# Layer-norm statistics: bf16 copy from GpSimd to ScalarE, square from ScalarE to VectorE

## What is computed

```python
x = x + 0.5 * ffn(_layernorm(x), Wg, We_gate, We_up, We_down, Ws_gate, Ws_up, Ws_down, Wsg)
x = x + attn(_layernorm(x), Wq, bq, Wk, bk, Wv, bv, Wo, bo)
x = x + 0.5 * ffn(_layernorm(x), ...)

def _layernorm(x, axis=-1, eps=1e-5):
    m = jnp.mean(x, axis=axis, keepdims=True)
    v = jnp.var(x, axis=axis, keepdims=True)
    return (x - m) / jnp.sqrt(v + eps)
```

## Time and profile before

| | us |
|---|---|
| median of three runs | 4568.49 |
| lowest, highest of the three | 4275.07, 4841.87 |
| the profiled execution | 4274.95 |
| its span, slowest core (core 2) | 4273.4 |
| spans of the eight cores | 4267.4 to 4273.4 |
| PE busy | 3931.2 |
| DVE busy | 2094.3 |
| ACT busy | 719.7 |
| POOL busy | 254.3 |

### The profile page before, as it was taken

One profiled execution on the slowest core, in us unless ns is written; L12 is line 12 of the kernel. 1 busy time (PEld: TensorE's weight loads), 2 busy tenths in 40 slices (PEclk: granted clock), 3 DMA queues, 4 the chain that ended last, 5 costly groups with the idle time before them and its releaser, 6 DMA issues.

```text
span 4273.4 us, 50465 instructions; the slowest of 8 cores (4267.4 to 4273.4 us)
## 1 busy us (share of the span) xinstructions
PE 3931.2 (92%) x17496; PEld 1592.7 (37%) x17496; DVE 2094.3 (49%) x3297; ACT 719.7 (17%) x1281; POOL 254.3 (6%) x390
## 2 busy tenths in 40 slices
PE   4699999999999999996878669999999999999999
PEld 1234444444444444431322223444444444444443
DVE  3545554445555555454334554555554445555544
ACT  3111111111111111113233321111111111111111
POOL 4100000000000000002000210000000000000000
PEclk7799999999999999997888779999999999999999
DMA  6023222232223222230020301321122211322112
GB/s 128 1 30 47 33 40 30 31 49 40 30 30 43 37 40 30 30 50 10 1 30 1 50 1 30 50 40 30 30 39 41 40 30 30 50 36 35 30 30 89
DMA packets 122599, 154.28 MB, mean 36 GB/s; under 512 B 3568, under 2 KB 93680, under 8 KB 122352
## 3 DMA queue, kind: packets, MB, share of 16 engines
q0 software_dynamic: 113744, 134.27, 21.1%
q1 hardware_dynamic: 6528, 12.59, 0.9%
q10 hardware_dynamic: 2080, 4.19, 0.3%
HBM read 276.91 MB, written 8.39 MB: 67 GB/s over the span
## 4 chain that ended last, share of the span: by engine, by line
PE 88%; DVE 5%; issue 3%; ACT 2%; DMA 1%; POOL 1%; DVEq 0%; ACTq 0%; POOLq 0%; SPq 0%
PE pb L534 27%; PE pb L576 27%; PE pb L558 26%; PE pb L657 1%; PE pb L824 1%; PE pb L646 1%; PE pb L567 1%; DVE t L393 1%; DVE rows L366 1%; DMA x_sb<-x_T 1%; DVE xn L397 1%; ACT t L757 0%; PE pb L343 0%; PE pb L348 0%; ACT t L760 0%
## 5 line engine op out<-in xcount | busy, mean ns | idle before, releaser
L534 PE MATMUL pb<-h_w,slab 128*128 128x512 bf16 x5120 | 1210.9, 378 | 41.5 <-DVE x_sb L539 4.4
L558 PE MATMUL pb<-xn,slab 128*128 128x512 bf16 x5120 | 1229.1, 384 | 0.0
L576 PE MATMUL pb<-xn,slab 128*128 128x512 bf16 x5120 | 1224.7, 382 | 0.0
L584 DVE TENSOR_TENSOR scr<-sg,w_sb 128x512 f32<-128x512 bf16 x640 | 442.8, 692 | 1280.7 <-ACT sg L581 1280.7
L539 DVE TENSOR_TENSOR x_sb<-x_sb,pb 128x512 f32<-128x512 f32 x1280 | 880.6, 688 | 345.2 <-PE pb L534 343.8
L558 PEld LDWEIGHTS pb<-xn,slab 128*128 128x128 bf16 x5120 | 505.2, 99 | 617.3 <-issue 26.4
L534 PEld LDWEIGHTS pb<-h_w,slab 128*128 128x128 bf16 x5120 | 433.6, 96 | 792.9 <-issue 412.9
L576 PEld LDWEIGHTS pb<-xn,slab 128*128 128x128 bf16 x5120 | 490.5, 98 | 612.0 <-issue 51.2
L581 ACT ACTIVATE sg<-pb 128x512 bf16<-128x512 f32 x640 | 381.3, 596 | 1315.9 <-PE pb L558 1315.8
L587 DVE TENSOR_TENSOR h_w<-scr,pb 128x512 bf16<-128x512 f32 x640 | 440.3, 688 | 163.4 <-PE pb L576 135.5
L572 ACT ACTIVATE w_sb<-pb 128x512 f32<-128x512 f32 x160 | 95.5, 597 | 1656.2 <-PE pb L567 1656.2
(11 more groups left out here) (116 smaller groups left out, 1032.3 us busy)
## 6 DMA issues: line engine op xcount, KB each, us to landing
slab<-WegT POOLq DMA_DIRECT2D x32, 1024.0 KB, 11.1
slab<-WeuT POOLq DMA_DIRECT2D x32, 1024.0 KB, 15.7
slab<-WedT POOLq DMA_DIRECT2D x32, 1024.0 KB, 9.5
slab<-WsgT POOLq DMA_DIRECT2D x8, 1024.0 KB, 11.0
slab<-WsuT POOLq DMA_DIRECT2D x8, 1024.0 KB, 15.1
slab<-WsdT POOLq DMA_DIRECT2D x8, 1024.0 KB, 9.2
out_T<-x_sb SPq DMA_DIRECT2D x4, 2048.0 KB, 7.1
x_sb<-x_T ACTq DMA_DIRECT2D x2, 2048.0 KB, 24.4
```

Source lines behind the costliest of these rows:

```text
L534: P.op("pe", lambda e, kc=kc, oc=oc, bd=bd, par=par: e.matmul(pb[bd][:, :], slab_d(4, kc, oc), h_w[:, par, kc, :], start=(kc == 0), stop=( ...
L558: P.op("pe", lambda e, sg_i=sg_i, kc=kc, hc=hc, t=t, bg=bg: e.matmul(pb[bg][:, :], slab_g(sg_i, kc, hc), xns(kc, t), start=(kc == 0), stop ...
L576: P.op("pe", lambda e, su_i=su_i, kc=kc, hc=hc, t=t, bu=bu: e.matmul(pb[bu][:, :], slab_g(su_i, kc, hc), xns(kc, t), start=(kc == 0), stop ...
L584: P.op("dve", lambda e, hc=hc: e.tensor_mul(t2f[:, :], sg[:, hc % 2, :], w_sb[:, :]), reads=[("sg", hc % 2), ("wsb",)], writes=[("scr32",)])
```

## The change

In `stats`, the bf16 copy of x moves from POOL to ACT, and the square moves from ACT to DVE, where it is made from the bf16 copy in `t2` instead of the float32 x. The buffers, their number, the matmuls and the recorded order stay.

```diff
-                    P.op("pool", lambda e, kc=kc, t=t, sl=sl: e.tensor_copy(
-                        t2[:, sl], xs(kc, t)),
+                    P.op("act", lambda e, kc=kc, t=t, sl=sl: e.activation(
+                        t2[:, sl], xs(kc, t), AF.Copy),
                         reads=[("x", kc, t)], writes=[tk])
-                    P.op("act", lambda e, kc=kc, t=t, par=par: e.activation(
-                        t1[:, par, :], xs(kc, t), AF.Square),
-                        reads=[("x", kc, t)], writes=[("t1", par)])
+                    P.op("dve", lambda e, kc=kc, sl=sl, par=par: e.tensor_mul(
+                        t1[:, par, :], t2[:, sl], t2[:, sl]),
+                        reads=[tk], writes=[("t1", par)])
```

## The result

The changed kernel takes 4318.2 us, the median of ten runs (lowest 4315.32); the kernel before, in ten runs beside it, 4275.33 (lowest 4274.72). The ratio is 1.0099, 95% interval 1.0087 to 1.0111: 1% slower, 43 us, and so within the 2% band. Forecast were 4317.0 and a range of 4290 to 4350. The profiled execution after took 4315.32 (span 4313.7, slowest core 6), 40.4 more than the 4274.95 of before (slowest core 2).

The account below looks back on a forecast made before the run. PE was seen busy 92% of the span, the change touching only three layer norms, each a chain over ACT and DVE. 12.5 + 3.4 + 3.1 + 22.8 = 41.8 us on 4274.95 gave 4317, range 4290 to 4350.

Parts of the forecast that it names:

- expert stages unchanged: Sign expected in the changed profile: the expert stages after the layer norms stay the same to a few us.
- The blocks, 22.8: Blocks 1 and 2 of each of three layer norms: row mathematics behind the multiplies, 3.8 us a block, 22.8 in all.
- The multiply at 0.42: Layer norms: each square on DVE takes 0.42 us with POOL idle, 0.87 as the upper end.
- Rival B: Layer norms: the DVE multiply takes 0.87 us, 16 us more than forecast, total 4333; chance 0.11.
- Block 0 in the attention and the second FFN, 3.4 and 3.1: Layer norms of attention and second FFN: the first root comes 3.4 and 3.1 us later, multiplies waiting behind DVE's residual add.
- Block 0 in the first FFN, 12.5: First layer norm: multiplies wait behind L310, so the root moves from 38.19 to 50.7 with a table load, 11.2 without.
- L310's place: Program start: DVE's first instruction, waiting for bias loads, moves from 32.63 to about 34.7 because early weight DMAs share bandwidth.
- the 4.1 us: Program start: q1 and q10's remaining 835 packets after 27 us, to the landing at 31.1; 6.2 with a third queue.
- rival C: Program start: the weights take more of the DMA engines, 6 us more, 4323, or up to 4354; chance 0.11.
- The stretches behind at no change: Stages after the three layer norms: no difference in length, 0 us in the sum.
- Rival A: Layer norms: not slower, since DVE is only 49% busy and the row mathematics stays hidden, 4275; chance 0.09.
- Rival D: Experts: longer gaps leave PE at its lower clock far in, slower by over 2%, 4360 and up; chance 0.04.

Follow-up runs that it names:

- e4: Changed kernel with the four DVE row operations L356 to L362 recorded one by one between the next block's multiplies: 4295.1 us, ratio 1.0048.
- e5: Kernel before with only the square moved to DVE, reading the bf16 copy, the cast staying on POOL: 4314.2 us, ratio 1.0091.
- e2: Changed kernel with the first weight slab DMA on POOL held until x's last block and the bias arrays have landed: 4305.8 us, ratio 1.0072.
- e11: Changed kernel with 12 added tiny DVE operations (copies of L310) ahead of expert 1's first token block in the first FFN: 4318.5 us, ratio 1.0099.
- e12: Changed kernel with 40 added tiny DVE operations (copies of L310) ahead of expert 1's first token block in the first FFN: 4321.2 us, ratio 1.0107.
- e6: Kernel before with only the cast moved to ACT, the square staying on ACT and reading float32 x: 4301.8 us, ratio 1.0061.

## Where the prediction was right, and which step failed

The forecast of 4317.0 lies 1.2 below the median and its direction, mechanism and places were right. That it lies so close is partly luck. The layer norms cost 4.1 more than forecast, and the stretches behind them, put at nothing, gave back 5.6. The step that failed in the layer norms is the price of the early weight DMAs, "With a third queue of equal share these become 6.2, so L310 runs at about 34.7": 2.1 us forecast, 5.5 measured. The step that failed behind them is "expert stages unchanged", with no term in the sum.

- **The blocks, 22.8.** Right. The six spacings that should grow did so by 4.07, 3.34, 3.47, 3.95, 4.05 and 3.40, 22.3 in all. Of each 3.8, the forecast had 2.8 for the row mathematics and 1.0 for the slower start and pace of the pairs; by the order alone e4 brought 16.7 of the 22.3 back, 2.8 a block, and 0.9 a block stayed. L356 stands right behind the last L340, as written.
- **The multiply at 0.42.** Right: 0.416 to 0.427 for all 96, with POOL not computing beside it; in e5, with POOL's casts there, the longest took 0.877. Rival B (0.87) is refuted.
- **Block 0 in the attention and the second FFN, 3.4 and 3.1.** Undersized: 4.4 and 4.2. The pace was taken as 0.66 us a pair; multiplies at 1948.63 and 1950.08 are 1.45 apart for two pairs, 0.72. The hand-overs (0.26 and 0.33 of idle DVE time) are longer than the 0.17 and 0.10 that I took.
- **Block 0 in the first FFN, 12.5.** 15.1 measured, from two errors. L310 came at 38.12 and not at 34.7; and the root needed no table load. The load at 17.61, before the first cast, had served both. With L310 3.4 later, 0.5 for the pace and 1.3 for the load not paid, the 50.7 of the forecast becomes 53.3. In the attention and the second FFN, behind the sigmoids, the root does pay its 1.28. The page "ScalarE: Activation LUTs" of the Trainium skill (section "Table sets: the hidden batching unit"), cited for a root in a set of its own, agrees with the trace there. In the first FFN what I drew from it was wrong, and not the page: with copies in every set, the load ahead of the first cast can be that of the root's set.
- **L310's place.** This is the failed step: +2.1 forecast, +5.5 measured. DMA queues of the changed kernel, 20 to 27 us, 27 to 33, then 27 to 60 (packets, MB, share of the 16 engines):

```profile
q1 hardware_dynamic: 493, 1.01, 49.0%
q10 hardware_dynamic: 493, 1.00, 39.8%
q0 software_dynamic: 496, 0.10, 17.3%
...
q0 software_dynamic: 273, 0.28, 36.6%
q1 hardware_dynamic: 269, 0.52, 35.5%
q10 hardware_dynamic: 271, 0.56, 30.8%
...
q0 software_dynamic: 3791, 4.34, 92.3%
q10 hardware_dynamic: 511, 1.01, 9.7%
q1 hardware_dynamic: 586, 0.59, 8.2%
```

  The equal share of three queues is there almost to the packet (273, 269, 271), and with it the rule that the forecast cited from the Trainium skill's page "DMA: Bandwidth & Descriptors" (section "Queues, rings and completion order") agrees. Two readings under the 4.1 us were wrong. First, the backlog: q1 and q10 still had 1097 packets and 1.60 MB to move at 27, where the earlier trace rows has 835 and 1.06. Most of this difference is not the change's: core 2, which the earlier trace rows shows, was ahead before any slab was issued (3.63 MB moved by 15 us, where the eight cores of before had 3.29 to 3.68 and core 6 had 3.36), and core 6 itself had 1.38 MB left at 27 before the change. Second, the weights were not at work from 27 only. Their first packets of q0 start at 24.4, and from 20 to 27 x moved 2.01 MB where core 6 had moved 2.14 before. From 27 on x got 1.08 MB in 6 us, 0.18 a us, where before the 1.06 took 4.1 us, 0.26 a us. On core 6 against itself L310 moved from 33.24 to 38.12, by 4.9, and e2 returned it to 32.62; it is e2 that shows the weights to be the cause. So rival C, "the weights take more", is true in its cause; its price over the forecast was 3.4 rather than 6. The forecast had this only as an upper end, with a sharing from 15 us on.
- **The stretches behind at no change.** Wrong by 5.6 in sum, 1.1 of it in the attention, which the mean over the cores does not bear out. In the FFNs two sources show in the traces. The long token blocks, 10 and 10 before, are 4 and 4 after, which is 0.8 and 2.1 us. And from the first L393 to the first L584 of the sixth token block the stages take 0.9 and 1.5 less: TensorE's granted clock rises at another point of the work. The second time that L558 runs in the second FFN, before and after:

```profile
2444.97 3.06 PE L558 MATMUL pb<-xn,slab 128*128 128x512 bf16 x8
```

```profile
2488.52 2.28 PE L558 MATMUL pb<-xn,slab 128*128 128x512 bf16 x8
```

  A group of eight takes 3.49 slow and 1.89 fast, so by 3.06 some 73% of the group ran slow before, and by 2.28 some 24% after; the granted clock over the two groups is 0.61 and 0.83. Neither source is work that the change moved; whether a shift by some other amount would bring or take such microseconds wasn't tried apart from e11 and e12.
- **Rival A** (hidden by a half-empty DVE) is refuted by the 3.33 us that ACT waits and by e4. **Rival D** (the slow clock far into the experts) is refuted: 0.98 in the window, as before, and each core's mean clock of 0.951 or 0.952 is 0.002 below before's, as layer norms that are longer and run at a lower clock would make it.

The sum of the measured terms is 40.3, against 41.8 forecast and 40.4 between the two profiled executions. The medians differ by 42.9; the profiled execution after was the lowest of its ten.

## What to carry to other kernels

Before moving work to an idle engine, look at that engine's queue and not at its share: a short operation that stands behind the moved work inherits all its waits, and the first instruction of an engine is a bad place for one that waits for a late load. An engine that is set free also starts its DMAs earlier, and these took bandwidth from the load that everything waited for. Where such a load is timed, look at several cores: by 15 us they differed here by up to 0.4 MB of x. Where a layer norm's root and reciprocal chain blocks to each other, recording them in the middle of the next block, so that another engine's work covers them, and putting the last one off into the next stage, brought 1.3% here.

## What the runs showed of the hardware that I had not expected

- ACT's 128x512 operations of 0.61 us start every 0.52 us when nothing holds them (e6). Durations in a timeline overlap; a stream's cost is read from its starts.
- A DVE operation on 128x8 values, 0.17 us long in L310's row, costs 0.27 us from start to start in a row of 40 (e12).
- A table load of 1.28 us ahead of the first cast made the first root free of one; behind the sigmoids of an FFN or the attention the root pays it.
- Single token blocks of the experts are 0.35 us longer than their like (22.2 against 21.86), every sixteenth of them, about 350.2 us apart, and at places that move with the program. Why is open.
